# Scatters of a recurrent gated mixture of experts on one core: other release points in the head, half pairs as release points in the pairs

## The reference

```
xn = layernorm(x)
s  = recurrent(xn): xn2 = layernorm(xn)*ln_w+ln_b; u = xn2@(Ws+Wi)^T + biases (16 states)
     h_t = tanh(A h_{t-1} + u_t);  s = (H@Wo^T + bo) * sigmoid(xn2@Wg^T + bg) + xn
g  = silu(moe(xn)): 16 experts, top 4 of sigmoid(xn@gate_w^T) + gate_b,
     weights = scores / their sum * 2.5;  expert: (silu(x@w1^T) * (x@w3^T)) @ w2^T
     plus one shared expert of the same form
out = x + s * g
```

## Time and profile before

| what | value |
|---|---|
| median of 3 runs | 521.76 us (520.88 to 526.37) |
| the profiled execution | 521.4 us |
| its span (first to last instruction) | 519.1 us |
| PE, DVE, ACT, POOL busy | 71%, 59%, 54%, 52% of the span |
| DMA queue share of 16 engines | 54.9% (SP's and ACT's), 20.5% (POOL's) |

### The profile page before, as it was taken

How to read it: one execution, slowest core, us unless ns; L and a number is a source line. 1 busy time by engine, 2 the same in 40 slices (tenths; PEclk the granted TensorE clock), 3 DMA queues, 4 the chain that set the end, 5 groups by cost and what they waited for, 6 DMA issues and landing times.

```text
span 519.1 us, 11521 instructions
## 1 busy us (share of the span) xinstructions
PE 367.0 (71%) x3635; PEld 292.8 (56%) x3635; DVE 307.6 (59%) x913; ACT 281.4 (54%) x532; POOL 268.3 (52%) x280
## 2 busy tenths in 40 slices
PE   0467389663999899789889879988879797843110
PEld 0354266342888788667677757767757676721000
DVE  4889697584342446634555447877635456637545
ACT  1842587573665656556767657666656565520000
POOL 2006757557005555565666546555544656526774
PEclk9999779997899999989999979999998999865555
DMA  7989879943577988698988869988877787645454
GB/s 237 386 289 310 296 256 331 342 144 119 176 231 236 333 289 267 200 291 260 302 264 280 287 197 290 285 272 233 287 224 212 249 274 229 205 130 152 141 154 130
DMA packets 106569, 127.06 MB, mean 245 GB/s; under 512 B 10257, under 2 KB 95890, under 8 KB 106514
## 3 DMA queue, kind: packets, MB, share of 16 engines
q1 hardware_dynamic: 92544, 92.17, 54.9%
q0 software_dynamic: 12288, 33.57, 20.5%
q10 hardware_dynamic: 1682, 0.59, 0.5%
HBM read 59.71 MB, written 66.58 MB: 243 GB/s over the span
## 4 chain that ended last, share of the span: by engine, by line
PE 41%; issue 15%; DVE 14%; SPq 7%; another core or an unknown queue 7%; POOL 6%; ACT 5%; DMA 3%; DVEq 0%; POOLq 0%; ACTq 0%
PE bank L741 16%; PE bank L764 10%; PE bank L565 6%; SPq L386 6%; POOL xn_parts L546 5%; PE bank L754 3%; PE bank L793 2%; PE bank L788 2%; DVE mix_sb L1141 1%; DVE xn_parts L1332 1%; DMA x_ring<-in_x 1%; DVE sh_h L1287 1%; DVE xn_f L1281 1%; DVE sh_silu L1295 1%
## 5 line engine op out<-in xcount | busy, mean ns | idle before, releaser
L525 POOL DMA_INDIRECT x_slots<-xn_parts,slot_u x128 | 132.9, 1038 | 148.0 <-PE bank L565 59.8
L546 POOL DMA_INDIRECT xn_parts<-y_slots,slot_u x128 | 128.4, 1003 | 96.0 <-PE bank L565 34.4
L741 PE MATMUL bank<-w_all,xn_f 128*128 x1038 | 134.5, 278 | 9.9 <-issue 9.0
L1281 DVE SCALAR_TENSOR_TENSOR xn_f<-bank,xn_f 128x256 f32<-128x256 f32 x88 | 36.8, 419 | 138.1 <-ACT xn_f L1605 76.8
L741 PEld LDWEIGHTS bank<-w_all,xn_f 128*128 128x128 f16 x1038 | 99.1, 101 | 29.4 <-issue 16.8
L1597 ACT ACTIVATE xn_f<-bank 128x1024 f16<-128x1024 f16 x88 | 88.5, 1007 | 25.7 <-PE bank L565 19.0
L1621 ACT ACTIVATE y_ring<-bank 128x512 f32<-128x512 f32 x88 | 52.0, 591 | 64.4 <-PE bank L764 34.2
L764 PE MATMUL bank<-w_all,sh_silu 128*128 x519 | 75.7, 283 | 9.4 <-ACT y_ring L1621 5.4
L565 PE MATMUL bank<-ident_h,w_stage 128*128 128x128 f16 x692 | 55.6, 225 | 8.6 <-DMA w_stage<-x_slots 8.6
L764 PEld LDWEIGHTS bank<-w_all,sh_silu 128*128 128x128 f16 x519 | 47.5, 102 | 18.4 <-issue 11.7
L565 PEld LDWEIGHTS bank<-ident_h,w_stage 128*128 128x128 f16 x692 | 48.1, 101 | 11.1 <-DMA w_stage<-x_slots 8.9
(11 more groups left out here) (173 smaller groups left out, 478.4 us busy)
## 6 DMA issues: line engine op xcount, KB each, us to landing
w_stage<-x_slots SPq DMA_DIRECT2D x85, 256.0 KB
y_slots<-y_ring SPq DMA_DIRECT2D x85, 256.0 KB
x_ring<-in_x SPq DMA_DIRECT2D x32, 256.0 KB
x_slots<-zero_h SPq DMA_DIRECT2D x1, 8064.0 KB, 30.5
x_slots<-zero_h SPq DMA_DIRECT2D x7, 1024.0 KB
x_slots<-zero_h SPq DMA_DIRECT2D x7, 768.0 KB
w_stage<-in_w13t SPq DMA_DIRECT2D x17, 256.0 KB
x_ring<-in_x SPq DMA_DIRECT2D x8, 512.0 KB
```

The source lines that it names most:

```text
L525: eng.indirect_dma_start(out=x_slots[s], out_offset=bass.IndirectOffsetOnAxis(ap=slot_u[:, n * TOPK + k:n * TOPK + k + 1], axis=0), in_=xn ...
L546: eng.indirect_dma_start(out=fin_y[:, r, j, k, :], out_offset=None, in_=y_slots[s], in_offset=bass.IndirectOffsetOnAxis(ap=slot_u[:, n * T ...
L741: mm = eng.matmul(gu[:, j * 2 * F:(j + 1) * 2 * F], xg_T[:, n % 2, ((j * 2 + px) * KD + k) * P:((j * 2 + px) * KD + k + 1) * P], w_all[:, ...
L1281: eng.scalar_tensor_tensor(out=h_sb[:, n % 2, 0:nb, :], in0=gv[:, 0:nb, F:2 * F], scalar=DESCALE, in1=silu_sb[:, n % 2, 0:nb, :], op0=ALU. ...
```

## The change

Three edits. (1) norm_scale(2), the roots of batches 4 and 5, moves on DVE from behind gates (0, 1) to ahead of shared_hidden(0). (2) The release points of segment 0's rows of three scatters from row 5 on alternate between sh_hidden of a batch (odd rows) and gate_pre of the second half of the batch before (even rows). (3) Segment 1's and 2's scatters and the gathers of units 0 to 11 are released by half pairs: an even half h is the transposes of a pair (pair_t of h // 2), an odd half the up product that PE issues right behind these transposes (pair_gu of h // 2 - 1, the product of the pair before). The starting pairs of the gathers and of the units' combines are moved by one pair or less.

```diff
-    SCATTER_PAIR = (0, 9, 29)
-    SCATTER_PAIRS = (0, 20, 16)
+    SCATTER_HALF = (0, 18, 58)
+    SCATTER_HALVES = (0, 40, 30)
...
-        UNIT_PAIR = (48, 52, 56, 60, 64, 68, 74, 78, 81, 85)
-        GATHER_PAIR = (45, 49, 53, 57, 61, 65, 70, 74, 77, 81, 84, 88)
-        GATHER_PAIRS = (8, 7)
+        UNIT_PAIR = (49, 53, 57, 61, 65, 69, 73, 77, 80, 84)
+        GATHER_HALF = (92, 100, 108, 116, 124, 132, 140, 147, 154, 161, 168, 175)
+        GATHER_HALVES = (8, 7)
...
-            steps = ((sh_silu_done, 1), (sh_hidden, 1), (gate_pre, 2), (x_hi, 5), (gate_pre, 3), (x_hi, 6), (gate_pre, 5),
-                     (x_hi, 7), (gate_pre, 7), (gate_pre, 8), (gate_pre, 9), (gate_pre, 10), (gate_pre, 11),
-                     (gate_pre, 13), (gate_pre, 14))
             def beside_gates(i):
-                if i and i % ROW == 0:
-                    made, count = steps[i // ROW - 1]
-                    eng.wait_ge(made, count)
+                row = i // ROW
+                if i % ROW or row == 0:
+                    return
+                if row == 1:
+                    eng.wait_ge(sh_silu_done, 1)
+                elif row == 2:
+                    eng.wait_ge(sh_hidden, 1)
+                elif row == 3:
+                    eng.wait_ge(gate_pre, 2)
+                elif row == 4:
+                    eng.wait_ge(x_hi, 5)
+                elif row % 2:
+                    eng.wait_ge(sh_hidden, (row - 1) // 2)
+                else:
+                    eng.wait_ge(gate_pre, row - 2)
+            def half_pair(h):
+                n = min(h // 2, NPAIR)
+                if h % 2 and h < 2 * NPAIR:
+                    eng.wait_ge(pair_gu, n - 1)
+                else:
+                    eng.wait_ge(pair_t, n)
...
-                            eng.wait_ge(pair_t, SCATTER_PAIR[s] + i * SCATTER_PAIRS[s] // (SEG_TILES[s] * TOPK))
+                            half_pair(SCATTER_HALF[s] + i * SCATTER_HALVES[s] // (SEG_TILES[s] * TOPK))
...
-                    if c < len(GATHER_PAIR):
+                    if c < len(GATHER_HALF):
                         i = k * FT + j
-                        eng.wait_ge(pair_t, min(GATHER_PAIR[c] + i * GATHER_PAIRS[s] // (2 * TOPK * FT), NPAIR))
+                        half_pair(GATHER_HALF[c] + i * GATHER_HALVES[s] // (TOPK * FT))
...
                 if b == 0:
                     norm_stats(4)
                     norm_stats(5)
+                    norm_scale(2)
...
                 gates(b, 1)
                 if b == 0:
-                    norm_scale(2)
                     norm_ratio(2)
```

## The result

The changed kernel takes 513.36 us in the median of 4 runs (510.54 to 516.38), beside it the kernel before 522.6 us: ratio 0.9852, 95% interval 0.9805 to 0.9899. That is 9.2 us less; forecast were 14.1 less (507.3). Two later jobs gave the same ratio (0.9842 and 0.9845). So the sign and the wide range (496 to 520) held; the forecast's own range (500 to 511) and the steps did not, as the rows show. One more thing has to be known for the experiments: in one job, on the chip that also ran another job at 524 us, the kernel before took only 471.18 us.

The account below looks back on a forecast made before the run. The head was taken to end with POOL's scatters, held back by release points, and pairs to lengthen with three or four POOL calls. 9.0 (2.4 + 4.6 + 2.0) + 5.1 = 14.1 us off 521.4 gave 507.3; range 496 to 520.

Parts of the forecast that it names:

- the head's 9.0: Head, up to pair 0: earlier roots, new release points and a shorter ACT stall together gain 9.0 us.
- the half pairs' 5.1: Expert pairs: spacing POOL's calls shortens three-call pairs by 2.2 us and four-call pairs by 2.9, together 5.1 us.
- rival B: Only the head gains, since POOL's calls in the pairs keep their number: 512.4 us; chance 0.22.
- Roots of batches 4 and 5: DVE in the head: norm_scale(2) moved earlier brings the whole chain of batches forward by 2.4 us, bounds 0 and 2.9.
- the low weights: Head: batch 0's low weights come 2.9 us later; if the loads SP then releases weren't hidden, the 2.4 us are lost.
- Even threes: Segment 0's last scatter rows on POOL: earlier release starts the last call 4.6 us earlier, bounds 3.3 and 5.1.
- The stall at 94: ACT's 6.1 us standstill in the head: rows come apart, six POOL calls in a row, not nine; 2.0 us gained.
- The 2.2 us of segment 1: Segment 1's scatters: three-call pairs cost 11.2 us extra in all; half-pair spacing wins back a fifth, 2.2 us.
- C: Only the last scatter rows of the head count; earlier norms bring nothing and ACT's stall stays: 516.8 us; chance 0.14.
- D: Pairs: half points join POOL's calls into runs of six, costing 4.4 us each: slower, 530 us; chance 0.10.
- E: Pairs: DVE's copy waits for POOL calls at the shared SBUF port, 42 us over 88 copies: 533 us; chance 0.02.

Follow-up runs that it names:

- head_second: Kernel before with only the moved norm_scale(2) and segment 0's new release points, pairs as before, at the higher level: 522.98 us, ratio 1.002.
- head_alone: Kernel before with only the moved norm_scale(2) and segment 0's new release points, pairs as before, at the lower level: 462.59 us, ratio 0.982.
- pauses_between_rows: Kernel after plus a memset nobody reads on POOL ahead of rows 4, 6, 8, 10, 12 and 14: 508.74 us, ratio 0.9678.
- halves_second: Kernel before with only the releases by half pairs, head as before, at the higher level: 514.08 us, ratio 0.9846.
- clumps_of_six: Kernel before with segment 2's scatters released six at a time, same number of calls, at the higher level: 532.93 us in one run.

## Why the prediction was right, and where it was wrong

The time fell inside the wide range, and the interval's end (0.9899) just below the bound of 1%, by a sum whose halves were both off: the head's 9.0 was nothing, the half pairs' 5.1 was rather more. That the two errors went opposite ways is luck. 513.4 also lies outside the forecast's own range (500 to 511) and 1 us from rival B's 512.4.

*Roots of batches 4 and 5, 2.4 us.* The roots started at 47.84 in place of 54.27, and the values of batch 4 came 3.2 us earlier (54.08 for 57.24). Alone, at the lower level, they moved pair 0 by 1.8. At the higher level the first stall stands behind them (69.17) and takes them back; the roots were not run alone there. My bound of 0 held, with the wrong culprit: I had named the low weights.

*Even threes, 4.6 us.* The last call was forecast at 118.5 and started at 119.28. But the step went on "PE (free at 120.1) and ACT are then no limit", at "unchanged points of the batches". That is where it failed: PE ended the gates at 129.41 (127.94 + 1.47), 9.3 us later than before and behind the third wait, and was the limit. Its last products for the shared expert took 4.54 us (123.57), at a granted clock of 0.58.

*The stall at 94, 2.0 us.* This is the step that failed. I had rows come apart, "six calls in a row, not nine (an estimate by the order on DVE)". Row 2 started late, at 51.86, behind the moved roots; the points of rows 3 to 5 were passed by the time POOL got to them, and 12 calls ran together. Three stalls of 17.45 us stand where one of 6.14 stood: 11.3 us lost, against the 9.0 that was to come; pair 0 on ACT came 1.1 later. head_second against head_alone shows that the same edits gain where no such wait stands, and pauses_between_rows shows that breaking the runs helps: nothing but pauses, and 3.7 us come back at pair 0.

The 9.0 itself was measured exactly at the lower level (125.6 to 116.6). Part of that is chance: there, roots gave 1.8 and not 2.4, the even threes 7.2 (123.8 to 116.6) and not 4.6, and the 2.0 for a stall can't have been earned, as there was none.

*Half pairs, 5.1 us.* The mechanism and its place were right, the size was at the low end. Alone they brought 6.9 us in the medians (514.08 for 520.96), and with the rest of the change 9.8 and 6.8 us between pairs 0 and 87, of bounds that went to 16.9. The two long pairs of before (6.08 us) are gone, but pair 80, with four calls, takes 6.0 us in the kernel after (5.3 before): long pairs did not vanish, as said. I had read only two four-call pairs, from the release points; by the times at which POOL got there nine pairs had four or more, and that is where more could be won. The 2.2 us of segment 1 lie between the 1.3 and 3.1 of pairs 0 to 29. One place was left out of the sum. The six gathers in a row ahead of pair 47 (5.01 us of wait) were read, but I counted "units 0 to 5" as having two a pair "and keep the number". Their number stayed; the half points parted them, and this wait went (29 to 47: 2.6 and 1.4 us). At the lower level the same edit gave 2.9 us, where there is no stall to remove.

*The rivals.* B (head alone) named the right sort of figure, 512.4 for 513.4, by the opposite parts, and halves_second and head_second refute it. C is refuted with it. D, calls that join and cost more than they bring, had the right mechanism in the wrong place: it happened in the head, not in the pairs, and clumps_of_six priced a run of six at 2.3 to 3.0 us where I had 4.4. Its sign came once, in part: where segment 1's scatters end and segment 2's begin, the kernel after has a run of five calls (237.52 to 243.65) and behind it on ACT

```profile
244.83 0.60 ACT L1639 ACTIVATE y_ring<-bank 128x512 f32<-128x512 f32 x1 [3.76 <-remote]
```

where the kernel before has four calls. Elsewhere from pair 8 to 439 us no run is longer than four. E: the copy L1313 keeps its durations, and DVE's idle time before it, where a copy that starts late would show, is 5.8 us in sum over 88 copies, beside 4.6 before; E had 42 us. The range of durations after, then the page's rows before and after:

```profile
L1313 DVE COPY sh_silu<-bank x88: 284/418/426, 139.9 to 451.8; 128x512 f16<-128x512 f16 x85, 128x256 f16<-128x256 f16 x3
...
L1295 DVE COPY sh_silu<-bank 128x512 f16<-128x512 f16 x88 | 36.2, 412 | 4.6 <-remote 4.6
...
L1313 DVE COPY sh_silu<-bank 128x512 f16<-128x512 f16 x88 | 36.4, 413 | 5.8 <-remote 5.1
```

The durations were 282/416/425 before, and the pairs became faster, not slower. The page SBUF — State Buffer of the Trainium skill (Who interferes with whom) also says that PE and ACT never wait on anyone. As far as it speaks of SBUF's ports no run here contradicts it, but it can't be read as a rule for POOL's neighbours at large: in head_second PE waits 1.1 us after every three transposes from 62 us to the end of POOL's run, and in head_alone, beside longer runs, it does not.

## What to carry to other kernels

On the occasions of 520 us, POOL's indirect calls in this kernel cost the other engines by how many followed each other without a pause, and not by their number alone; at 471 us they did not. So count the longest run before and after, row by row, and from the time at which POOL really gets there, since a row that starts late finds its neighbours' points passed. Moving release points earlier can lengthen a run; a pause on POOL (a half point in the pairs, even useless work in the head) can pay for itself. And measure the parts on the same occasion: here one and the same edit was worth 9 us on one and nothing on another.

## What was not expected of the hardware

**Runs of indirect DMAs slow PE and ACT.** In the jobs of 520 us, each run of 9 or 12 calls in the head that began after 50 us came with a wait of 4.7 to 8.4 us on ACT, that ended 1.0 to 1.9 us behind the run. Its size does not follow the length alone: the run of 12 from 52 us cost 7.7 to 8.4 us, those from 99 to 105 us 5.0 to 5.1. Nine calls from 44.87 to 58.63 in halves_second, with 0.40 us ahead of the fourth, had no such wait. Runs of six cost 2.3 to 3.0 us each in the pairs (one run).

**Two levels.** The kernel before took 521 to 524 us in four jobs and 471.18 us in one (22 runs), on a chip that also gave 524.32. The table lays the same kernel at both levels side by side (head_alone and head_second), by stretches of the table above:

| stretch | lower | higher |
|---|---|---|
| first scatter of segment 0, start | 39.2 | 39.2 |
| from there to pair 0 | 77.4 | 93.4 |
| pairs 0 to 8, no call of POOL | 26.1 | 25.0 |
| pair 8 to the tail | 268.5 | 315.9 |
| tail, to the last instruction | 50.0 | 49.9 |

Where POOL makes no calls the two are alike to 1.1 us, and so is the tail, in which PE and ACT are busy for 6.6 and 4.0 us of the 50 (POOL 34.3, DVE 27.0). All of the difference lies where POOL's calls stand beside PE's and ACT's work. PE's granted clock was lower there, 0.85 for 0.93 from the first scatter to pair 0 and 0.95 for 0.99 from pair 8 to the tail, and PE was busy for 68.3 in place of 57.5 us and 262.5 in place of 248.3. So a slower PE can stand for at most 10.8 of the 16.0 us and 14.2 of the 47.3; the rest is time in which PE did nothing, and the rows above show a low clock right behind such time. At the lower level the waits behind runs are missing, not merely shorter, so it is not one slower clock for everything. The DMA queues give no reason: 61.1% of 461.2 us and 54.6% of 523.3 us are 282 and 286 us of packet time on SP's and ACT's queue. The page Runtime: NRT & Kernel Launch of the Trainium skill (Instruction fetch mechanics) says that fetching the next block of instructions is mostly hidden; the two profiles have the same 34 packets on one such queue, at 0.5% and 0.4% of the span, so these rows don't point to it; nor do they show how long PE waited for a block of instructions, so they don't rule it out. What sets the level, and by what way POOL's calls reach PE's and ACT's issue, stays open. The whole change was not run at the lower level; 459.6 us there (471.2 - 8.6 - 3.0) is only a sum.
